# Eleven pieces of the second layer's first keys and values made beside combination and normalisation

## The reference, cut to what matters

```python
x = x + jnp.tanh(g_xattn[0]) * _L0_xattn_ref(_layernorm(x), ctx_1024, ctx_1024, mask, ...)
x = x + jnp.tanh(g_ffn[0]) * _L0_ffn_ref(_layernorm(x), ...)      # 64 experts, 8 chosen, and a shared one
x = x + jnp.tanh(g_xattn[1]) * _L1_xattn_ref(_layernorm(x), ctx_1024, ...)
x = x + jnp.tanh(g_ffn[1]) * _L1_ffn_ref(_layernorm(x), ...)      # 8 experts, 2 chosen, and a dense one

# _L1_xattn_ref, 16 heads of 32
q = _split_heads(query_tokens @ Wq + bq)
k = _split_heads(key_value_tokens @ Wk + bk)
v = _split_heads(key_value_tokens @ Wv + bv)
probs = jax.nn.softmax(einsum(q, k) / sqrt(32)); ctx = einsum(probs, v) @ Wo + bo
```

## Time and profile before

| | us |
|---|---|
| median of 3 runs | 2293.46 |
| lowest and highest | 2284.22, 2298.40 |
| profiled execution, its time | 2298.78 |
| its span | 2296.7 |
| PE busy in the span | 2116.5 (92%) |
| DVE, ACT, POOL busy | 1286.3, 1027.2, 522.9 |
| TensorE clock granted, mean | 0.963 |

### The profile page before, as it was taken

The page is one execution under the profiler, slowest core; times in us unless marked ns, Lnnn a source line. Parts: engine busy times, 40 slices in busy tenths (PEclk is TensorE's granted clock), DMA queues, the critical chain, the costliest instruction groups (busy, mean ns, idle before and its releaser), DMA issues. The chain is left out here.

```text
span 2296.7 us, 39535 instructions
## 1 busy us (share of the span) xinstructions
PE 2116.5 (92%) x13342; PEld 1497.4 (65%) x13343; DVE 1286.3 (56%) x2759; ACT 1027.2 (45%) x2377; POOL 522.9 (23%) x501
## 2 busy tenths in 40 slices
PE   6999999998998999999579999999899979999995
PEld 4777777776944444444257777777678437777773
DVE  4677777767572222222356777777640127777775
ACT  2566666655211111111135666666542016656663
POOL 3000000002354554555330000000024002333231
PEclk9999999998999999999789999999889989999997
DMA  7000000010145999999430000000112046665552
GB/s 281 27 33 32 32 32 32 7 77 30 62 169 191 326 333 325 335 310 278 98 129 27 28 27 27 27 27 1 75 71 69 10 197 245 241 233 208 187 187 71
DMA packets 65436, 292.78 MB, mean 127 GB/s; under 512 B 10066, under 2 KB 10236, under 8 KB 45972
## 3 DMA queue, kind: packets, MB, share of 16 engines
q1 hardware_dynamic: 45572, 251.34, 29.2%
q0 software_dynamic: 19728, 39.62, 8.0%
HBM read 259.62 MB, written 37.06 MB: 129 GB/s over the span
## 5 line engine op out<-in xcount | busy, mean ns | idle before, releaser
L728 ACT ACTIVATE probs<-ps,less_max 100x360 f32<-100x360 f32 (+1 forms) x384 | 212.0, 561 | 162.7 <-DVE less_max L582 88.3
L1547 PE MATMUL pgu<-ring,xT 128*128 x560 | 267.1, 600 | 5.4 <-issue 2.8
L714 ACT ACTIVATE pTs<-pt 128x300 f32<-128x300 f32 x512 | 189.3, 425 | 125.6 <-PE pt L476 124.4
L1547 PEld LDWEIGHTS pgu<-ring,xT 128*128 128x128 f32 x560 | 100.0, 192 | 112.5 <-issue 112.2
L476 PE MATMUL pt<-ident,probs 100*128 100x100 f32 (+1 forms) x1152 | 137.6, 257 | 28.5 <-ACT pTs L714 26.4
L1904 DVE TENSOR_TENSOR ws_low<-w,ws_high 128x2048 fp32r<-128x2048 f32 x63 | 143.2, 2292 | 24.2 <-ACT ws_high L1835 24.2
L476 PEld LDWEIGHTS pt<-ident,probs 100*128 100x128 f32 (+1 forms) x1152 | 116.5, 141 | 58.9 <-issue 36.0
L349 PE MATMUL po<-first 128*128 128x362 f32 (+1 forms) x768 | 147.2, 341 | 3.0 <-PEq L184 2.5
L353 PE MATMUL pp<-first 128*128 128x512 f32 x576 | 146.1, 402 | 2.3 <-DVE first L377 2.3
L353 PE MATMUL po<-first 128*128 128x512 f32 (+1 forms) x576 | 145.1, 401 | 0.0
L349 PE MATMUL pp<-first 128*128 128x360 f32 (+1 forms) x768 | 143.6, 336 | 1.4 <-DVE kT_low L371 1.2
(11 more groups left out here) (301 smaller groups left out, 4212.0 us busy)
## 6 DMA issues: line engine op xcount, KB each, us to landing
ring<-in_l_ew SPq DMA_DIRECT2D x64, 1536.0 KB, 8.5
w<-in_l_ew SPq DMA_DIRECT2D x64, 1024.0 KB, 7.8
xnT<-in_ctxT SPq DMA_DIRECT2D x14, 1444.0 KB, 6.5
first<-in_l_up SPq DMA_DIRECT2D x2, 4096.0 KB, 13.6
b<-in_l_eb SPq DMA_DIRECT2D x8, 1024.0 KB, 4.6
moe_sum<-zrow SPq DMA_DIRECT2D x3, 2048.0 KB, 15.4
moe<-moe_sum SPq DMA_DIRECT2D x24, 200.0 KB
wd<-in_l_down SPq DMA_DIRECT2D x2, 2048.0 KB, 7.9
```

What stands on the lines that cost most here:

```text
L714: act.activation(pTs[:, g % 2, j, 3 * half:3 * half + 3, :].rearrange("k c q -> k (c q)"), pt[:, half, 0:3 * S], ACT.Copy).then_inc(t_out, 1)
L728: act.activation(probs[g % 2 * HPC + j][:, k0:k1], ps[j][0:S, 0:k1 - k0], ACT.Exp, bias=less_max[:, g, seg, j:j + 1], scale=-1.0 if masked ...
L1547: last = pe.matmul(pgu[p][:, :], xT[p][:, c, :], wgu[c], start=c == 0, stop=c == DC - 1)
```

## The change

- In `experts_swiglu`, SP issues behind the last weights of the experts five loads: the raw context of batch 0, the raw key and value weights, the key bias and the query weights. ACT makes the three high parts of the context between its two last `y`, and the two high parts of the weights behind the last; DVE makes the low parts behind its last step of the experts.
- `clear_semaphores` moves from behind the combination to ahead of it.
- `combine` and `layer_norm` become one block for this seam, `combine_and_normalise`. PE makes 11 of the 14 pieces of batch 0 there, in four banks, and then the transposes. ACT makes `kT` high and copies the pieces of values, and only then takes the root. DVE makes `kT` low of one piece ahead of each of the first six batches; each batch is added, its statistics taken and aggregated in one go; the last two pieces of keys stand between the statistics and the reciprocal.
- The projection block of layer 1 has no splits; the head of layer 1 has three pieces left, `("v", 3)` to `("v", 5)`, in a new order of steps.
- Layer 0 computes as before.

```diff
+SPLIT = ((0, 256), (256, 512), (512, SK))
+MADE_AHEAD = (("k", 0, 0), ("k", 0, 1), ("k", 1, 0), ("k", 1, 1), ("k", 2, 0), ("k", 2, 1), ("v", 0), ("v", 1),
+              ("k", 3, 0), ("k", 3, 1), ("v", 2))
...
-        SPLIT = ((0, 256), (256, 512), (512, SK))
+        ahead = layer == 1
...
+            if ahead:
+                wq = env.wq_ahead
+            else:
+                wq, wk_raw, wv_raw = (cq.enter_context(nc.sbuf_tensor(env.name(n), [P, DC, D], F32))
+                                      for n in ("wq", "wk_raw", "wv_raw"))
+                kv_in = [env.semaphore(n) for n in ("wk_in", "wv_in")]
+                first_raw = cq.enter_context(nc.sbuf_tensor(env.name("first_raw"), [P, DC, SK], F32))
+                first_in = env.semaphore("first_in")
+                layer_norm(nc, env, (
+                    (wq[:, :, :], w_q, wq_in), (bq[:, :], b_q, wq_in), (wk_raw[:, :, :], w_k, kv_in[0]),
+                    (wv_raw[:, :, :], w_v, kv_in[1]), (first_raw[:, :, :], env.ctxT[0], first_in)), env.inputs)
...
-                    pe.wait_ge(wq_in, 32)
+                    if not ahead:
+                        pe.wait_ge(wq_in, 32)
...
-                        if n in (1, 3):
+                        if not ahead and n in (1, 3):
...
+                if ahead:
+                    pe.sem_inc(piece_mm, len(MADE_AHEAD))
+                    scores(0, 0, 0, 0, True)
+                    scores(0, 0, 0, 1)
+                    first_piece("v", 3)
...
+                for n, (there, src) in enumerate(((env.raw_ahead[2], env.ctxT[0]), (env.raw_ahead[0], env.kv_ahead[0]),
+                                                  (env.raw_ahead[1], env.kv_ahead[1]))):
+                    sp.dma_start(there[:, :, :], src).then_inc(raw_in[n], 16)
+                sp.dma_start(env.bk_ahead[:, :], env.kv_ahead[2]).then_inc(rest_in, 16)
+                sp.dma_start(env.wq_ahead[:, :, :], env.kv_ahead[3]).then_inc(rest_in, 16)
+                sp.wait_ge(rest_in, 32)
...
+                act.wait_ge(raw_in[0], 16)
+                for k0, k1 in SPLIT:
+                    act.activation(env.mid_first[0][:, :, k0:k1], env.raw_ahead[2][:, :, k0:k1], ACT.Copy)\
+                        .then_inc(ctx_high, 1)
                 last_pair = last_pair_of(act)
                 row_out(last_pair * 2 + 1, last_pair, 1)
+
+                for n in range(2):
+                    act.wait_ge(raw_in[n + 1], 16)
+                    act.activation(env.wide_first[2 * n][:, :, :], env.raw_ahead[n][:, :, :], ACT.Copy).then_inc(w_high, 1)
...
+                for n, (k0, k1) in enumerate(SPLIT):
+                    dve.wait_ge(ctx_high, n + 1)
+                    dve.tensor_tensor(env.mid_first[1][:, :, k0:k1], env.raw_ahead[2][:, :, k0:k1],
+                                      env.mid_first[0][:, :, k0:k1].bitcast(F32), ALU.subtract)
+                for n in range(2):
+                    dve.wait_ge(w_high, n + 1)
+                    dve.tensor_tensor(env.wide_first[2 * n + 1][:, :, :], env.raw_ahead[n][:, :, :],
+                                      env.wide_first[2 * n][:, :, :].bitcast(F32), ALU.subtract)
...
+def combine_and_normalise(nc, env):
...
+        NB = 4
+        pk = [cx.enter_context(nc.psum_tensor(env.name(f"pk{n}"), [P, 512], F32)) for n in range(NB)]
+        pT = [cx.enter_context(nc.psum_tensor(env.name(f"pT{n}"), [P, DC, S], F32)) for n in range(2)]
...
+            @block.tensor
+            def _(pe):
+                for i, what in enumerate(MADE_AHEAD):
+                    if i >= NB:
+                        read = MADE_AHEAD[i - NB]
+                        pe.wait_ge(*((k_out, K_AHEAD.index(read) + 1) if read[0] == "k" else (v_out, V_AHEAD.index(read) + 1)))
+                    for c in range(DC):
+                        for n, m in PARTS:
+                            first, last_one = c == 0 and (n, m) == PARTS[0], c == DC - 1 and (n, m) == PARTS[-1]
+                            if what[0] == "k":
+                                g, (k0, k1) = what[1], SEG[what[2]]
+                                last = pe.matmul(bank_of(what)[:, 0:k1 - k0], wk[n][:, c, g * P:(g + 1) * P],
+                                                 ctx[m][:, c, k0:k1], start=first, stop=last_one)
+                            else:
+                                kc = what[1]
+                                last = pe.matmul(bank_of(what)[:, :], ctx[n][:, c, kc * P:(kc + 1) * P], wv[m][:, c, :],
+                                                 start=first, stop=last_one)
+                    last.then_inc(made, 1)
+                for t in range(B):
+                    pe.wait_ge(xn_done, t + 1)
+                    if t >= 2:
+                        pe.wait_ge(copied, t - 1)
+                    for c in range(DC):
+                        last = pe.transpose(pT[t % 2][:, c, :], xn[:, t, c * P:(c + 1) * P], ident[0:S, 0:S])
+                    last.then_inc(turned, 1)
+            @block.scalar
+            def _(act):
+                for i, what in enumerate(MADE_AHEAD):
+                    act.wait_ge(made, i + 1)
+                    if what[0] == "k":
+                        g, (k0, k1) = what[1], SEG[what[2]]
+                        act.activation(kT[0][:, g, k0:k1], bank_of(what)[:, 0:k1 - k0], ACT.Identity, bias=bk[:, g:g + 1])\
+                            .then_inc(k_high, 1)
+                    else:
+                        act.activation(v0[:, what[1], :], bank_of(what)[:, :], ACT.Copy).then_inc(v_out, 1)
+                act.wait_ge(var_done, B + 1)
+                act.activation(std[:, :], stats[:, :, 0], ACT.Sqrt).then_inc(std_done, 1)
+                for t in range(B):
+                    act.wait_ge(turned, t + 1)
+                    act.activation(xnT[:, :, t * S:(t + 1) * S], pT[t % 2][:, :, :], ACT.Copy).then_inc(copied, 1)
+            @block.vector
+            def _(dve):
+                def keys_low(n):
+                    g, (k0, k1) = K_AHEAD[n][1], SEG[K_AHEAD[n][2]]
+                    dve.wait_ge(k_high, n + 1)
+                    dve.scalar_tensor_tensor(out=kT[1][:, g, k0:k1], in0=bank_of(K_AHEAD[n])[:, 0:k1 - k0],
+                                             scalar=bk[:, g:g + 1], in1=kT[0][:, g, k0:k1].bitcast(F32),
+                                             op0=ALU.add, op1=ALU.subtract).then_inc(k_out, 1)
+                for t in range(B):
+                    if t < 6:
+                        keys_low(t)
+                    dve.wait_ge(sums_in[t], 16 * len(moe))
+                    dve.tensor_tensor(moe[0][:, t, :], moe[0][:, t, :], moe[1][:, t, :], ALU.add).then_inc(added_up, 1)
+                    dve.wait_ge(added_up, t + 1)
+                    dve.scalar_tensor_tensor(out=x[:, t, :], in0=moe[0][:, t, :], scalar=gate, in1=x[:, t, :],
+                                             op0=ALU.mult, op1=ALU.add).then_inc(x_done, 1)
+                    dve.wait_ge(x_done, t + 1)
+                    dve.bn_stats(stats[:, t, :], x[:, t, :]).then_inc(stats_done, 1)
+                    dve.wait_ge(stats_done, t + 1)
+                    dve.bn_aggr(mv[:, t, :], stats[:, t, :]).then_inc(var_done, 1)
+                dve.wait_ge(var_done, B)
+                dve.tensor_scalar(stats[:, :, 0], mv[:, :, 1], EPS, None, ALU.add).then_inc(var_done, 1)
+                keys_low(6)
+                keys_low(7)
+                dve.wait_ge(std_done, 1)
+                dve.reciprocal(rstd[:, :], std[:, :]).then_inc(rstd_done, 1)
+                dve.wait_ge(rstd_done, 1)
+                for t in range(B):
+                    dve.tensor_scalar(xn[:, t, :], x[:, t, :], mv[:, t, 0:1], rstd[:, t:t + 1],
+                                      ALU.subtract, ALU.mult).then_inc(xn_done, 1)
...
+                if layer == 0:
+                    clear_semaphores()
+                    combine_and_normalise(nc, env)
+                else:
+                    combine(nc, env, layer)
...
-        clear_semaphores()
```

292 lines of the change are left out of this document (185 added, 107 removed).

## The result

| | before | after |
|---|---|---|
| median of 20 runs, us | 2296.15 | 2285.60 |
| lowest and highest | 2284.22, 2302.50 | 2280.31, 2290.88 |
| profiled execution, its time | 2298.78 | 2288.45 |

The ratio is 0.9955, with a 95% interval of 0.9946 to 0.9964: faster by 0.45%, which the 20 runs of each kernel tell from no change at all, and within the 1% that the prediction called no change. The forecast was 2284.8 us. That it lies 0.8 us from the median is in part luck: it was reckoned from a median before of 2293.46 us (3 runs), which is 2296.15 us in 20 runs, so the medians differ by 10.6 us where 8.7 were forecast.

A forecast was written before the change was run, and what follows sets the result against it. PE was taken as the bound from the projection on and idle 17.8 us in combination. Projection start +7.5 us and head -16.2 us gave -8.7 us, so 2293.5 became 2284.8 us; range 2273 to 2297.

The forecast's parts named there:

- The bound and the offer: PE idle 17.8 us in combination, the bound from the projection on; moving head pieces there gives at most 25.8 us.
- The end of the experts, +2.0: First load of the sums (T) later: 0.6 us from ACT's context splits delaying the last `y`, 1.4 from the moved clear.
- The rule of the Trainium skill that I weighed: At the experts' end, DVE splits could start POOL's last addition up to 1.2 us later; left out of the sum.
- Combination and normalisation, T + 31.0: Normalising starts 31.0 us after the first load of the sums (T): PE's pieces until 28.3, then copy, table load, root, reciprocal.
- DVE a hair ahead of PE: In combination, DVE's batches and low parts end at T + 27.7, T + 29 with the last two; PE's 28.3 is the term.
- The clock is down again after the gap: PE's 3.2 us idle ahead of the transposes drops its clock; projection starts 7.5 us later, +3.3 us shift if it stayed up.
- The head, -16.2: Layer 1's attention start (A) to the fifth maxima takes 28.1 us, bound by scores, maxima and exponentials, partly at low clock.
- from the loop on everything is as before: Behind the head, from the attention loop on, the change was taken to alter no time.
- that the clock holds: Rival: clock stays up over the 3.2 us gap and the head's gaps; -14.7 us, 2278.8 us; chance 0.15.
- That it is down all along: Rival: low clock in normalisation, projection, head and the loop's first steps; -0.3 us, 2293.2 us; chance 0.22.
- The pieces slow to their end: Rival: pieces in combination run at 1.2 GHz throughout, taking 51.6 us, 23.6 more; kernel at 2307 us; chance 0.05.
- Loads that hurt the last tiles: Rival: the five loads delay the experts' last tiles; priced at nothing, 2 us for a gather 13 us late; no separate chance.

The follow-up runs named there:

- e5: The changed kernel with no piece made ahead, all 14 pieces in the head in the order of before; ratio to before 1.0005.
- e2: The changed kernel with ten pieces ahead instead of eleven, piece (v, 2) made in the head between the first two sets of scores; ratio to before 0.9953.
- e1: The changed kernel with ACT's root of the variances ahead of the last piece's copy instead of behind it; ratio to before 0.9939.
- e4: The changed kernel with 26 matmuls that nobody reads filling PE's waits in the head of layer 1; ratio to before 0.9948.
- e7: The changed kernel with e1's early root and e4's unread matmuls in the head together; ratio to before 0.9931.
- e8: e7 with DVE's low parts behind its batches instead of ahead, the last two behind the normalised batches; ratio to before 0.9904.
- e10: e2 (ten pieces ahead) with DVE's low parts behind its batches as in e8, no unread matmuls; ratio to before 0.9933.
- e3: The changed kernel with 16 matmuls that nobody reads between the last piece and the first transpose; ratio to before 0.9929.
- e9: e1 (early root) with DVE's low parts behind its batches as in e8, no unread matmuls; ratio to before 0.9901.

## Why the prediction was right, step by step

- **The bound and the offer**: shown. Without pieces there is no gain (e5), with them PE works where it did nothing.
- **The end of the experts, +2.0**: measured +1.90. The splits' overhang delays the last `y` by 0.33 us, against 0.6; POOL's slow copy adds 0.25; and from the last addition to T there are 10.64 us instead of 9.32, +1.32, which answers to the clear (1.4). The weight splits and the five loads cost nothing that a mark shows. The rule of the Trainium skill that I weighed (SBUF — State Buffer, section "SBUF: two separate sides") has a row here, POOL's copy at 1.51 instead of 0.76 us beside DVE's splits. Three quarters of a us on the copy became 0.25 us on the path, so leaving it out of the sum was a small error, a fifth of the 1.2 us that I had worked out for it.
- **Combination and normalisation, T + 31.0**: measured T + 29.33; the mechanism was right, PE's pieces and then the row of steps behind them, and the size 1.7 us too long. The pieces took 26.9 us instead of 28.3: PE started 0.05 us behind T and not 0.3, a piece of keys takes 1.99 us (two in 1151.35 to 1155.34) and not the 2.09 that I read as the distance of two starts in the head, two pieces of values take 5.56 and the last 2.94 and not 3.02 each; the low clock cost 2.4, against 2.2. The row behind them took 2.4 instead of 2.7. (By the sum's own terms the sixth piece starts at T + 13.0 and not at the 13.9 that stands there; it started at T + 12.4 and no bank was awaited.)
- **DVE a hair ahead of PE**: it ended 0.5 us behind PE, 1.7 ahead of the reciprocal. Its batches were aggregated at T + 26.2 and its last low part out at T + 27.4, where I had 27.7 and 29. So DVE was not what normalising waited for; e2 shows it as the bound, at T + 27.7. That moving the root gets most of this difference I had not seen.
- **The clock is down again after the gap**: right, with a gap of 3.03 us for 3.2. It was low in the projection for 5.7 us, and before for 4.3 (4.5 put down); half of the difference is the +0.67. That the clock was worth 2.0 + 2.2 us here is borne out by e1: 1.67 and 2.81.
- **The head, -16.2**: measured -15.95, by two errors that cancel. The chain at full clock is 24.9 us and not 26.3: a step takes 3.80 us and not 4.3 (e4, its second scores at 1204.41 and its first at 1200.61), since the maxima start 0.80 behind the scores and not 1.2, and the first exponential 0.57 behind those and not 0.8. By the fourth maxima that makes 0.9 us (A + 16.8 in e4, 17.7 put down), and the stretch behind them is 0.5 shorter than reckoned. The low clock costs 3.5 us and not the 1.8 that I had placed between the ends. PE was busy for 68% of the head, where I had put under 65%. And "from the loop on everything is as before" was not so: the 1.1 us up to the sixth maxima are a cost that the sum lacks.
- **Rivals**: that the clock holds did not happen in this kernel, but up to the head it is what e1 is, and in the head as well e7 and e8; there the sum of the marks fell by 17.4 to 19.6 us against before, 1.8 to 2.3 us of it by the earlier start of normalising, where I had -14.7. That it is down all along: the head was 28.4 and not 34.5. By the Trainium skill's rule (TensorE: Matmul & The Clock Gate, section "A second HAM failure mode: psum-queue depth-cycling") idle times between groups of matmuls lose the time in the swings of the clock; the trace agrees as to the mechanism (0.51 from 1200 to 1205, and 3.5 us back when e4 closes the gaps), and its price in the head, 3.5 us, is a third of the 10.8 by which the sum of the marks fell from e5 to the change. The pieces slow to their end: the clock was up 5.3 us after T. (Its 2307 does not follow from its terms, which give 2284.8 + 23.6 = 2308.4.) Loads that hurt the last tiles: no mark shows it.

## What to carry to other kernels

Work of a bound engine that moves into another engine's stretch is worth what it frees at its old place, less what of it outlasts its new cover; price the new place by what stands in a row behind its last piece, and look there for a table load or a root that waits for nothing but its turn. Where PE then works in groups with waits between them, price each wait twice, once as itself and once as the clock for the dense work behind it, and look for an instruction whose place shortens the wait before thinking of more work. What a small gap at the edge of a block does to the clock went both ways here in kernels alike at that place, so one profiled execution does not settle it. And let the marks run on until the clock of both kernels is the same again: here 1 to 1.5 us lay just behind the last one.

## What was not expected of the hardware

- A gap of 3.03 us ahead of the transposes brought PE's clock down, and so did 3.67 us (e10) and 3.83 us (e2); with 1.88 us (e7), 1.57 us (e1) or 0.87 us (e8) it stayed up. When it fell differed: in the kernel after while PE still waited, in e4, with the same 3.03 us, and in e10 only when the transposes had begun. Once down it stayed at 0.50 through 7 us of transposes in which PE was busy for 6.30 of 7.75 us, and 5.7 us of dense projection.
- At the end of the block, with 0.85 us between two blocks and transposes that kept PE busy for two thirds of 6.13 us, it fell in two executions (e3, e9) and not in three (e1, e7, e8).
- The table load goes as soon as its turn comes, ahead of the wait of its own instruction: in e1 at 1154.63, while the root waited until 1156.65. What stands ahead of it in ACT's order decides whether it is hidden.
- POOL's eight additions of the bias to `x` took 9.84 us with DVE's splits gone from beside them, and 15.99 us before: the earlier trace rows and the window of after have the busy times, 17.56 and 11.42 us with the scaling of the bias. Nobody waited for them in either.
